# Embedding interaction and tower on one core: field tiles in the order 0, 1, 4, 2, 3, and field 12 picked by matmul in all halves

## The reference

```
e = stack([tbl_f[ids[:, f]] for f in range(16)], axis=1)      # (2048, 16, 16)
A  = repeat(x0, 16, axis=1)                                   # (b, 16*39, 16)
Bm = repeat(e, 39, axis=2).reshape(b, 16*39, 16)
z  = einsum('bnh,bnd,nk,khd,kd->bkh', A, Bm, alpha, w, hv)    # (b, 16, 16)
h  = concat([z.reshape(b, 256), dense_ctx], axis=1)
h  = relu(h @ W_top1 + b_top1)                                # 272 -> 512
h  = relu(h @ W_top2 + b_top2)                                # 512 -> 256
y  = h @ W_top3                                               # 256 -> 1
```

## Time and profile before

| | |
|---|---|
| median of three runs | 341.95 us |
| profiled execution | 345.54 us |
| its span | 341.80 us |
| TensorE busy | 189.8 us, 2626 matmuls |
| VectorE busy | 152.3 us |
| GpSimd busy | 111.2 us, 120 instructions |
| ScalarE busy | 74.3 us |
| HBM read | 32.28 MB |

### The profile page before, as it was taken

The page is one execution under the profiler, slowest core; times in us unless marked ns, Lnnn a source line. Parts: engine busy times, 40 slices in busy tenths (PEclk is TensorE's granted clock), DMA queues, the critical chain, the costliest instruction groups (busy, mean ns, idle before and its releaser), DMA issues. The chain is left out here.

```text
span 341.8 us, 6034 instructions
## 1 busy us (share of the span) xinstructions
PE 189.8 (56%) x2626; PEld 137.7 (40%) x2626; DVE 152.3 (45%) x179; ACT 74.3 (22%) x201; POOL 111.2 (33%) x120
## 2 busy tenths in 40 slices
PE   6423000000000120011598899999999999999996
PEld 2311000000000010000386488787777778786764
DVE  5500000000000304000008989999999999978520
ACT  5300000000000100000242631434253523232222
POOL 4777777777777777740000000000000000000000
PEclk9999999999999999999999899999999999999999
DMA  4896910000000000500000427656565665640000
GB/s 104 298 230 210 246 11 7 7 7 6 6 7 7 7 8 6 129 5 0 2 0 4 142 107 190 233 146 207 187 204 177 182 241 128 249 123 2 2 0 0
DMA packets 14699, 32.70 MB, mean 96 GB/s; under 512 B 6620, under 2 KB 10569, under 8 KB 11593
## 3 DMA queue, kind: packets, MB, share of 16 engines
q1 hardware_dynamic: 9579, 31.04, 30.1%
q0 software_dynamic: 3712, 0.96, 3.1%
q10 hardware_dynamic: 1382, 0.34, 0.5%
HBM read 32.28 MB, written 0.05 MB: 95 GB/s over the span
## 5 line engine op out<-in xcount | busy, mean ns | idle before, releaser
L398 POOL DMA_INDIRECT e<-tbl_dram,ids_all x116 | 111.0, 957 | 38.5 <-issue 35.0
L490 DVE TENSOR_TENSOR prod<-x,bank 128x2048 f32<-128x2048 f32 x40 | 90.9, 2280 | 29.3 <-remote 17.1
L426 DVE TENSOR_REDUCE e<-bank 128x32 f32<-128x96 f32 (+2 forms) x30 | 9.7, 381 | 134.0 <-remote 98.1
L744 PE MATMUL bank<-consts,e_cols 128*128 128x128 f32 x80 | 15.0, 303 | 80.1 <-issue 80.1
L415 DVE TENSOR_SCALAR onehot<-ids_b 125x2304 bf16<-125x2304 f16 (+3 forms) x88 | 50.6, 624 | 7.5 <-ACT ids_b L523 6.1
L714 PE MATMUL bank<-parts,onehot 125*128 125x48 bf16 x1240 | 41.8, 186 | 13.1 <-issue 10.9
L714 PEld LDWEIGHTS bank<-parts,onehot 125*128 125x128 bf16 x1240 | 38.1, 98 | 20.7 <-issue 12.8
L744 PEld LDWEIGHTS bank<-consts,e_cols 128*128 128x128 f32 x80 | 11.0, 194 | 82.5 <-issue 82.3
L552 ACT COPY e_cols<-e 128x128 f32<-128x128 f32 x80 | 18.6, 303 | 106.6 <-issue 101.9
L756 PE MATMUL bank<-prod,m_w 128*32 128x256 f32 x640 | 39.2, 386 | 0.0
L690 PE MATMUL bank<-tower,w 128*128 128x256 f32 x128 | 32.2, 386 | 0.5
(11 more groups left out here) (50 smaller groups left out, 82.8 us busy)
## 6 DMA issues: line engine op xcount, KB each, us to landing
x<-x_dram SPq DMA_DIRECT2D x16, 1024.0 KB
x<-x_dram SPq DMA_DIRECT2D x16, 512.0 KB
ids_b<-ids_half_dram SPq DMA_DIRECT2D x4, 576.0 KB, 7.3
e<-tbl_dram,ids_all POOLq DMA_INDIRECT x116
prod<-windows_c_dram SPq DMA_DIRECT2D x1, 768.0 KB
prod<-windows_c_dram SPq DMA_DIRECT2D x1, 512.0 KB
w_z<-w_z_dram SPq DMA_DIRECT2D x1, 512.0 KB
w<-w_dram SPq DMA_DIRECT2D x1, 512.0 KB
```

What stands on the lines that cost most here:

```text
L398: nc.gpsimd.indirect_dma_start(out=e[:, tile, f * D:(f + 1) * D], out_offset=None, in_=t[f"tbl_{f}"][:, :], in_offset=bass.IndirectOffsetO ...
L490: nc.vector.tensor_tensor(prod[:, s % NPROD, :].rearrange("p (q b) -> p q b", q=HP), x0[:, tile % NX, :].rearrange("p (q b) -> p q b", q=H ...
L744: made = nc.tensor.transpose(win_bank[j][:, i * HB + bt * P:i * HB + (bt + 1) * P], src, ident)
```

## The change

The steps of a half handle the units in the order 0, 1, 4, 2, 3. The fills of windows are now j = 0 (units 0, 1), j = 1 (unit 4), j = 2 (units 2, 3). Gathers and x tiles come in that order. `HOT` begins with 4 and has 12 in the middle; field 12 is picked in all halves, fields 13 and 15 are gathered in half 7. The third pack of tables with its late parts is gone. The products of steps 0 and 1 are contracted at step 2, half 1's planes are made at steps 1 and 2, and the last half contracts as the others do.

```diff
-HOT = [12, 1, 2, 5, 4, 7, 10, 13, 15]
-LATE, LATE_FROM = HOT[0], 2
+HOT = [4, 1, 2, 5, 12, 7, 10, 13, 15]
 N_FIRST = 4
+N_LAST = 7
-PACKS = [HOT[1:1 + N_FIRST], HOT[1 + N_FIRST:], [LATE]]
+PACKS = [HOT[:N_FIRST], HOT[N_FIRST:]]
-SIZES = [(0, 4, 10), (4, 9, 8)]
+SIZES = [(0, 1, 8), (1, 5, 10), (5, 9, 8)]
+def end_hot(n):
+    return N_LAST if n == NH - 1 else len(HOT)
+def hot_with(k, lo, hi):
+    having = [j for j in range(lo, hi) if KT[HOT[j]] > k]
+    return having[0], having[-1] + 1
-FILL_OF = [0, 0, 1, 1, 2]
-FILL_UNITS = [[0, 1], [2, 3], [4]]
+UNIT_OF = [0, 1, 4, 2, 3]
+FILL_OF = [0, 0, 1, 2, 2]
+FILL_STEPS = [[0, 1], [2], [3, 4]]
+FILL_BLOCKS = [[0, 1], [4], [2, 3]]
-TILE_LOADS = [1, 1, 2]
+TILE_LOADS = [1, 2, 1]
-GATHERED = [... for fs in ([0, 1, 2, 3, 4, 5, 6], [7, 8, 9, 10, 11, 12, 13], [14, 15])] for n in range(NH)]
+GATHERED = [... for fs in ([0, 1, 2, 3, 4, 5, 6], [13, 14, 15], [7, 8, 9, 10, 11, 12])] for n in range(NH)]
...
-    _steps = range(1, 2) if _n == 1 else ...
+    _steps = range(1, 3) if _n == 1 else ...
-JOBS = {BEFORE: [("ids", n, j) for n in range(2) for j in range(1, len(HOT), 2)]}
+JOBS = {BEFORE: [("ids", n, j) for n in range(2) for j in range(0, len(HOT), 2)]}
-IDLE_TURNS = {(0, 1): 16, (0, 2): 4, (1, 0): 14}
-CONTRACTS = {1: [0, 1], 3: [2], 4: [3], 5: [4]}
-for _n in range(1, NH - 1):
+IDLE_TURNS = {(0, 1): 4, (0, 2): 16, (1, 0): 14}
+CONTRACTS = {2: [0, 1], 3: [2], 4: [3], 5: [4]}
+for _n in range(1, NH):
     CONTRACTS[UH * _n + 3] = [UH * _n, UH * _n + 1, UH * _n + 2]
     CONTRACTS[UH * _n + 5] = [UH * _n + 3, UH * _n + 4]
-for _s in range(UH * (NH - 1), STEPS):
-    CONTRACTS[_s + 1] = [_s]
+        TABLES_LEFT = [(slice(KT_AT[HOT[N_FIRST]], ...), o_bank[1][...]), (slice(KT_AT[HOT[N_FIRST + 1]], KT_ALL), z_bank[...])]
...
 # SyncE
-            load_table(2)
-            sp.wait_ge(gathered[0][1], 16 * 2 * len(GATHERED[0][1]))
+            sp.wait_ge(gathered[0][2], 16 * 2 * len(GATHERED[0][2]))
 # ScalarE, at each step
-                if g in (0, 2):
-                    spread_e(n, FILL_OF[g + 2])
+                if n == NH - 1:
+                    if g == 0:
+                        spread_e(n, 2)
+                elif g == 0:
+                    spread_e(n, 1)
                 elif g == 3 and n + 1 < NH:
                     spread_e(n + 1, 0)
...
+                if s == 1:
+                    spread_e(n, 2)
                 for job in jobs:
                     empty(job)
-                if s in (2, 3):
-                    keep_part(2, s - 1)
+                if g == 1 and 0 < n < NH - 1:
+                    spread_e(n, 2)
                 if s in IDS_REL:
                     take_row_off(IDS_REL[s])
+                if s == UH * (NH - 1) - 1:
+                    spread_e(NH - 1, 1)
 # TensorE: remainders of the second pack in two pieces
-                pe.wait_ge(table_split, 3 + n + 1)
-                nc.tensor.matmul(table_left, neg_ident[:], parts[:, ks, n, :], ...).then_inc(table_rest, 1)
+                pe.wait_ge(table_split, 3 + n + 1)
+                for ks, left in TABLES_LEFT:
+                    made = nc.tensor.matmul(left, neg_ident[:], parts[:, ks, n, :], ...)
+                made.then_inc(table_rest, 1)
 # TensorE, at each step
-                if s == 1:
-                    for unit in CONTRACTS[1]:
+                if s == 2:
+                    for unit in CONTRACTS[2]:
                         contract(unit)
-                    for plane in PLANES[1][:FIRST_PICKS]:
+                    for plane in PLANES[1]:
                         pick_rows(*plane)
-                if g in (1, 3):
-                    turn_windows(n, FILL_OF[g + 1])
+                if n == NH - 1:
+                    if g < 2:
+                        turn_windows(n, g + 1)
+                elif g in (1, 2):
+                    turn_windows(n, g)
                 elif g == 4 and n + 1 < NH:
                     turn_windows(n + 1, 0)
```

More of the change, by code:

```diff
@@ L67 @@
 Y_TILES, QT = 4, 32
-GATHERED = [[[f for f in fs if f not in HOT[first_hot(n):]] for fs in ([0, 1, 2, 3, 4, 5, 6], [7, 8, 9, 10, 11, 12, 13], [14, 15])] for n in range(NH)]
-FILL_PACK = [max([p for p, pack in enumerate(PACKS[:2]) for f in pack if f < top]) for top in (7, 14, 16)]
+GATHERED = [[[f for f in fs if f not in HOT[:end_hot(n)]] for fs in ([0, 1, 2, 3, 4, 5, 6], [13, 14, 15], [7, 8, 9, 10, 11, 12])] for n in range(NH)]
+FILL_PACK = [max([p for p, pack in enumerate(PACKS[:2]) for f in pack if f < top]) for top in (7, 16, 16)]
 def _windows():
@@ L93 @@
 EC = max(window_start(f) for f in range(8 * FT)) + CW
+assert max(window_start(f) for f in range(16)) + CW <= 7 * D and min(window_start(f) for f in range(32, F)) >= 13 * D
 AT_IDENT, AT_H_MASK, AT_K_MASK, AT_ROW = 0, P, 3 * P, 3 * P + K
@@ L119 @@
 PLANES_BY = {n: max(at for at, plane in enumerate(ALL_PLANES) if plane[0] == n) + 1 for n in range(NH)}
-FIRST_PLANES = sum(lo == 1 for n, lo, hi, k in ALL_PLANES if n == 0)
+FIRST_PLANES = sum(n == 0 and lo < N_FIRST for n, lo, hi, k in ALL_PLANES)
 def kept_at(n, p):
@@ L264, in program @@
         in_win = [sem(f"in_win_{n}") for n in range(2)]
-        in_table = [sem(f"in_table_{p}") for p in range(3)]
+        in_table = [sem(f"in_table_{p}") for p in range(2)]
         in_tower = sem("in_tower")
@@ L420, in keep_rows @@
                 for p in packs:
-                    for first, places, fields, apart in SUM_RUNS[p]:
-                        if SUMS[p][first] == LATE and n < LATE_FROM:
-                            continue
+                    for first, places, fields, apart in (SUM_RUNS if n < NH - 1 else LAST_RUNS)[p]:
                         src = bass.AP(o_bank[p], first * D, [[512, P], [3 * SUM_W, 2], [fields * D, places], [1, fields * D], [SUM_W, 3]])
@@ L543, in spread_e @@
                     act.wait_ge(win_turned, fill_at(n - 2, j) + 1)
-                if n == 0 and j == 2:
+                if n == 0 and j == 1:
                     act.wait_ge(padded, 1)
-                for ft in range(2 * j, min(2 * j + 2, FT)):
+                for ft in FILL_BLOCKS[j]:
                     base, inner = WINDOWS[ft]
@@ L575, in keep_part @@
                 else:
[L576 to L578 removed]
+                    act.wait_ge([first_left, table_rest][p], n)
+                for ks, left in [(ks, table[:, ks, :])] if n == 0 else [(ks, first_rest[n - 1])] if p == 0 else TABLES_LEFT:
+                    made = nc.scalar.copy(parts[:, ks, n, :], left)
+                made.then_inc(table_split, 1)
             def keep_z(n):
@@ L783, in _ @@
             for _ in range(6):
-                nc.tensor.matmul(win_bank[0][:], zeros[:, 0:P], zeros, start=True, stop=True)
+                nc.tensor.matmul(win_bank[0][:], zeros[:, 0:P], zeros[:], start=True, stop=True)
             pe.wait_ge(pick_made, 1)
@@ L832, in _ @@
                         fill_t(job)
-                if s > 1 and s != 4:
+                if s > 1 and s not in (2, 4):
                     for unit in CONTRACTS.get(s, []):
@@ L847, in _ @@
                         pick_rows(*plane)
+            contract(CONTRACTS[STEPS][0])
             fill_t(JOBS[STEPS][0])
-            for unit in CONTRACTS[STEPS]:
-                contract(unit)
+            contract(CONTRACTS[STEPS][1])
             for job in JOBS[STEPS][1:]:
```

107 lines of the change are left out of this document (50 added, 57 removed).

## The result

The changed kernel takes **356.72 us** (median of 4 runs, 354.96 to 357.91), the kernel before 342.47 beside it (4 runs, 341.65 to 343.68): a ratio of 1.041, interval 1.037 to 1.045. It is slower, by 14.2 us. The forecast was 352, range 346 to 362.

What follows compares the result with a forecast made beforehand. TensorE was taken as the bound: a slow stretch sets the start, then TensorE's work fills the rest. 0.2+2.9+8.2-0.9-0.3 = +10.1 us on 345.54 gives 355.6; the median, 3.6 lower, gives 352, range 346 to 362.

Steps and rivals of the forecast that it cites:

- The sum: Whole kernel: all terms together add 10.1 us, giving 352 us for the median, range 346 to 362.
- Halves 1 to 6: Turn j = 2 on TensorE waits for ScalarE's four copies behind two relus: +1.36 us a half, +8.2 in all.
- Start: Before the first tower matmul: 20 more picks and extra id jobs delay half 1's picks, +2.9 us, bounds +0.9 to +5.
- slow stretch: TensorE's early part, records 0.7 to 2.1 us apart until about 167; extra records there were to cost +0.2 us.
- The block in VectorE: Half 0's last plane waits for TensorE, products of steps 0 and 1 behind it: hidden, 4.5 us if uncovered.
- Gathers 0: GpSimd's queue keeps 116 gathers and its end, and SyncE's new order of loads delays nothing: zero cost.
- Picks and tail: Half 7 has 32 fewer picks, -0.9 us; changes from step 35 on give -0.3 us.
- Rival 1: Slow stretch ends by records, not time: eight more records cost +5.6 to +10.4 us, 358 to 362.5; chance 0.11.
- Rival 2: TensorE's clock falls in the new waits of six halves: +4 to +6 us, 356 to 358; chance 0.09.
- Rival 3: Slow stretch shortens as two products and an x tile leave it, 17 us earlier: 335; not slower 0.13, faster 0.07.

Runs made afterwards that it cites:

- the last run: The changed kernel with copies early, the twentieth plane behind products 0 and 1, and fields 13 and 15 picked in the last half too: 341.75 us, ratio 0.9975.

## Why the prediction was right, point by point

**The sum: right in direction and range, 4.7 us too low.** Forecast 352, measured 356.72. Of the 4.7, 0.5 is that before's median is 342.47 and not 341.95, and 1.1 is in the terms (the marks give +11.2 for +10.1). The other 3.1 lies between the median runs and the two profiled executions, whose spans differ by less than the medians do; no trace here says where it lies.

**Halves 1 to 6: the mechanism was right, the size too low.** Forecast 8.2 (1.36 a half), measured 1.64 under each of halves 1 to 4 of the table. TensorE stands 1.80 us (253.23 to 255.03), not 1.69, since it is released 0.14 us behind the end of the copies (254.89) and not 0.04, and the four turns take 0.72 to the start of layer 2, not 0.56: 1.80+0.72+1.73 = 4.25 in place of 3.98. That gives 1.63. The five runs with early copies, the turn-late run and the old order are without the stop; the two runs that keep the copies late keep it. That shows the cause.

**Start: right in sum, by two errors against each other.** Forecast +2.9 and +0.2, measured +2.29. From the first picks of half 0 behind the stretch to the first tower matmul it is 33.91 us in after (169.06 to 202.97) and 30.24 before (170.44 to 200.68), so this work costs +3.67, inside the bounds of 0.9 to 5. The path was as forecast: VectorE's reduction starts 2.05 us later (193.27 for 191.22), the record behind the stop 2.31 (196.19 for 193.88), the first tower matmul 2.29. Against it, those picks start 1.38 us earlier: the window sums were done inside the slow stretch in after, and at its end before. With the old fields in the new order it is 31.57 us (182.07 to 213.64), so of the 3.67 some 1.3 belongs to the order and 2.3 to the choice of fields, to which the prediction gave the 20 picks and the id jobs. A part that the prediction's term lacks is the clock. In after and in that run the contraction of steps 0 and 1 comes behind a thinly filled stretch and runs below full clock; with the old fields that costs 1.2 us, nearly the 1.3 of the order (one profile each):

```profile
188.70:193.20 4.50, 2.68 (x17) 1.60 (x16) 2.54 (x5) 4.42 (x14) 0.00 (x0) 1.00 0.01 2
193.20:196.30 3.10, 3.10 (x34) 1.29 (x34) 3.10 (x4) 0.82 (x2) 0.00 (x0) 0.60 0.02 5
```

(The contraction takes 3.12 us there, 1.93 before.) In after it costs 0.8 in the contraction and, as an estimate from 90 picks in 3.07 us and 70 in 1.93 at full clock, 0.6 in the picks behind it. Where before takes 200 us the first tower matmul comes 6.0 us later with the new fields in the old order, 5.2 of them behind the first picks, and which piece costs that isn't settled: this run and the changed kernel on the same chip have a stop of 2.19 and 2.16 us that no event explains.

**The block in VectorE** was said to be hidden, with 4.5 as its price uncovered. It was, where before takes 342 us: taking it away brought no earlier mark.

**Gathers 0: not quite.** GpSimd's last gather starts at 152.22 in after and at 148.96 before, since it stood 3.54 us for its second set of ids at 25.47. SyncE issues them behind the two loads of the third unit's x tile. The prediction had GpSimd's queue keep its end and put SyncE's new order at zero, looking only at who waits for x and not at who waits for the ids behind it. TensorE is at full pace 1.4 us later.

**Picks and tail.** Forecast -0.9 and -0.3; the last three marks give +1.03+2.41-1.07, which less two stops of 1.64 is -0.9 for -1.2.

**Rival 1** (the stretch ends by records) would have put full pace 5.6 to 10.4 us later; it came at 169.06 for 167.69. (What it held against this rival, a pace that rises forty-fold, sets a record beside a matmul; matmul beside matmul it is 2.6 us against 0.030, nearly ninety-fold.) **Rival 2** (the clock falls in the new waits) is out for the six halves: the granted clock of 247.0 to 267.32 is 1.00, around a stop of 1.80 us between full stretches. The rule of the Trainium skill, "TensorE: Matmul & The Clock Gate", Part 1, cited for it, is that recent activity lifts the clock, and the trace agrees in both places: full clock where TensorE works 18.50 of 20.32 us, and 0.69 behind 2.88 of 4.90 us in the start, where the prediction hadn't looked for it. **Rival 3** (the stretch shortens) is out: the products left it and it ended 1.4 us later, and with the products ahead of it or behind it (28.99 or 169.72) it ends within 0.1 us of the same time (169.04 and 169.06). What the prediction left unnamed, the gathers behind the stretch, is in the last section.

No version beats both kernels beyond doubt. Where before takes 200 us, fewer picks in the last half gives 0.9% without an interval. Where it takes 342, the last run is at 0.9975. The eight more gathers that help where there is no slow stretch are what makes the stretch longer where there is one.

## What to carry to other kernels

Before a copy is made the releaser of a transpose, look at what its engine has queued ahead of it: two relus and four copies stood between TensorE and work that was ready, and moving one call gave back 12 us of 14. A count of operations that stays the same can still move in time, so compare the last issue of each queue, not its length. And when an engine crawls through a stretch and nothing releases it, halve the work of whoever is busy beside it: it costs one run, on a chip that shows the stretch.

## What the runs showed of the hardware

**The same program takes 342 us or 200 us.** Of the four chips that ran experiments two had the slow stretch in all 17 runs of the kernel before and two had it in none. Each was used once, so whether it goes with the chip or with the time and place isn't shown. The difference lies before the first tower matmul (200.68 us with the stretch, 56.06 and 57.18 without it for the same order and the same start); from there on the periods are the same to 0.01 us.

**The slow stretch follows GpSimd's gathers.** Start of the last gather, start of full pace on TensorE, and difference (us), where the stretch exists:

```
half of the gathers (60)          78.95    90.89   11.9
all picked (112)                 146.62   162.83   16.2
before (116)                     148.96   167.69   18.7
plane behind products (116)      152.11   169.04   16.9
after (116)                      152.22   169.06   16.8
old fields, last gathered (124)  159.40   179.20   19.8
```

A line through the six (a fit of these rows, with 90.89 as the latest it can be) has the stretch end at 7.9 us and 1.38 for each gather, within 0.8 of every row; GpSimd issues one every 1.25. So the end seems not to be a fixed time behind the last issue, but to move by a little more than the issue does.

In it TensorE's records start at multiples of 0.7 us from each other (165.56, 166.26, 167.66, 168.36, 169.06 in after), SyncE's issues at 1.4 (33.25, 34.66, 36.05, 37.45 before), and the idle time is put down to "issue". Fewer gathers end it sooner even where that means more picks. It isn't the gathers' data that TensorE waits behind at the end. Of the kernel before, all DMA traffic from 151 to 167 us:

```profile
DMA packets 0, 0.00 MB, mean 0 GB/s; under 512 B 0, under 2 KB 0, under 8 KB 0
```

The Trainium skill, "Perfetto Trace Analysis", under "DMA Instruction — SWDGE (GPSIMD)", says that a gather's reported end is that of its descriptors and not of its data. By that rule the data could run on behind 150 us; the row shows that it doesn't. What holds TensorE up while gathers are issued and some 12 to 20 us behind them stays open, and so does why two chips are free of it: there GpSimd issues the same gathers (the changed kernel's last one at 159.40) while TensorE has worked at full pace since 26 us. Every run here was timed with its records taken, so whether taking them plays a part isn't shown either.

**The granted clock says nothing of the pace in the slow stretch.** It is 0.51 through that of after (30.6 to 165 us) and 1.00 through that of before, with much the same pace in both (1.40 us a record in after, 1.30 before). Behind the stretch it does count: the same 14 idle transposes, behind the same stop of 2.4 us, take 2.50 us at 0.66 and 3.25 at 0.50 (after, and the plane-behind-products run).
